# First batch loaded beside the weights, first routed group fetched in the first stage's drain

## What is computed

```python
h = tok_ref(x)                      # x[128, 375, 512]: q, k, v of 125 channels each, softmax over 512
h = h + attn_ref(layernorm(h), Wq, Wk, Wv, Wo)         # 8 heads of 64, 2 of keys and values, rope, tanh cap
h = h + ffn_ref(layernorm(h), gate_w, w1, w2, w3, sw1, sw2, sw3, expert_bias)

def ffn_ref(x, ...):                # 16,000 tokens, 8 experts, top 2, hidden width 448
    scores = softmax(xf @ gate_w); sel = top_k(scores + expert_bias, 2)
    order = argsort(flat_sel, stable=True); token_idx = order // 2
    routed_in = xf[token_idx] * top_scores_sorted[:, None]
    h = silu(ragged_dot(routed_in, w1, counts)) * ragged_dot(routed_in, w3, counts)
    out = silu(xf @ sw1) * (xf @ sw3) @ sw2
    return out.at[token_idx].add(ragged_dot(h, w2, counts))
```

## Time and profile before

| | us |
|---|---|
| median of 3 runs | 5829.84 |
| lowest, highest | 5828.87, 5832.68 |
| the profiled execution | 5829.3 |
| its span | 5827.5 |
| PE busy | 5695.0 (98%) |
| DVE busy | 4158.4 (71%) |
| ACT busy | 3372.5 (58%) |
| POOL busy | 2001.2 (34%) |
| mean granted PE clock | 0.991 of full speed |

### The profile page before, as it was taken

One profiled execution on the slowest core, in us unless ns is written; L12 is line 12 of the kernel. 1 busy time (PEld: TensorE's weight loads), 2 busy tenths in 40 slices (PEclk: granted clock), 3 DMA queues, 4 the chain that ended last, 5 costly groups with the idle time before them and its releaser, 6 DMA issues. The chain is left out here.

```text
span 5827.5 us, 109798 instructions
## 1 busy us (share of the span) xinstructions
PE 5695.0 (98%) x32259; PEld 5030.8 (86%) x32259; DVE 4158.4 (71%) x9591; ACT 3372.5 (58%) x6260; POOL 2001.2 (34%) x1711
## 2 busy tenths in 40 slices
PE   5999999999999999999999997999999999999999
PEld 4888888888888888888888885899999999999998
DVE  3777777777777777777777775676777677667675
ACT  4666666666666666666666663555555555555554
POOL 1333333333333333333333332333333333333333
PEclk8999999999999999999999998999999999999999
DMA  2111111111111111111111111777777777777762
GB/s 74 45 49 48 44 48 49 44 48 49 44 47 50 44 46 50 45 46 50 45 45 50 46 45 45 190 190 188 184 187 189 185 188 188 190 185 186 188 167 80
DMA packets 363663, 565.45 MB, mean 97 GB/s; under 512 B 92898, under 2 KB 187106, under 8 KB 363492
## 3 DMA queue, kind: packets, MB, share of 16 engines
q1 hardware_dynamic: 294276, 433.22, 24.9%
q0 software_dynamic: 69344, 131.70, 11.4%
HBM read 438.14 MB, written 138.42 MB: 99 GB/s over the span
## 5 line engine op out<-in xcount | busy, mean ns | idle before, releaser
L1435 POOL DMA_INDIRECT out_dram<-res,goal x273 | 483.9, 1773 | 1135.8 <-DMA entries<-routed_entries 476.2
L945 POOL TENSOR_TENSOR vT_low<-vT_full,vT_high 128x500 fp32r<-128x500 f32 x128 | 162.6, 1271 | 1576.5 <-ACT vT_high L691 1576.5
L624 ACT ACTIVATE e<-ps,negmax 128x512 f32<-128x512 f32 x512 | 350.6, 687 | 427.4 <-PE ps L437 416.0
L1182 PE MATMUL ps<-rT_hi,up_hi 128*128 128x384 f32 x2548 | 552.2, 338 | 6.5 <-DVE rT_lo L1345 6.5
L1182 PE MATMUL ps<-rT_lo,up_hi 128*128 128x384 f32 x2548 | 551.6, 338 | 0.0
L1182 PE MATMUL ps<-rT_hi,up_lo 128*128 128x384 f32 x2548 | 551.4, 338 | 0.0
L1275 ACT ACTIVATE uT_hi<-egb 128x384 fp32r<-128x384 f32 x364 | 191.4, 526 | 572.0 <-DVE egb L1364 523.6
L966 POOL DMA_INDIRECT routed_entries<-entry,slot x256 | 320.3, 1251 | 468.4 <-DVE slot L906 425.9
L1182 PEld LDWEIGHTS ps<-rT_hi,up_hi 128*128 128x128 f32 x2548 | 457.2, 188 | 14.3 <-issue 6.8
L1182 PEld LDWEIGHTS ps<-rT_lo,up_hi 128*128 128x128 f32 x2548 | 456.1, 188 | 0.0
L1182 PEld LDWEIGHTS ps<-rT_hi,up_lo 128*128 128x128 f32 x2548 | 456.1, 188 | 0.0
(11 more groups left out here) (220 smaller groups left out, 14993.9 us busy)
## 6 DMA issues: line engine op xcount, KB each, us to landing
raw<-in_L_ffn_w SPq DMA_DIRECT2D x182, 768.0 KB, 5.1
X<-in_x SPq DMA_DIRECT2D x128, 750.0 KB
raw<-in_L_ffn_w SPq DMA_DIRECT2D x91, 896.0 KB
raw<-in_L_ffn_w SPq DMA_DIRECT2D x273, 128.0 KB, 5.4
normed_rows<-y SPq DMA_DIRECT2D x128, 250.0 KB
out_dram<-h SPq DMA_DIRECT2D x128, 250.0 KB
rows<-normed_rows,entries POOLq DMA_INDIRECT x273, 4.0
out_dram<-res,goal POOLq DMA_INDIRECT x273
```

Source lines behind the costliest of these rows:

```text
L624: nc.scalar.activation(e[:, i, :], ps[:, (i + 1) % 2, :], ACT.Exp, bias=negmax[:, i:i + 1], accum_out=total[:, i:i + 1]).then_inc(e_sb.sem, 1)
L1182: ins = nc.tensor.matmul(ps[:, bank, 0:GROUP], w[a][:, k, col:col + P], rT[b][:, k, :], start=(k == 0 and i == 0), stop=(k == KC - 1 and i ...
L1435: nc.gpsimd.indirect_dma_start(out, bass.IndirectOffsetOnAxis(ap=goal[group[1] % 2][:, i:i + 1], axis=0), res[i][:], None, bounds_check=la ...
```

## The change

It has two halves, and some buffers move for them.

**Start.** SP's first DMA is now batch 0 of `x`. The loads of the weights follow in the old order, `raw_q` in two DMAs of 512 KB in place of eight of 128 KB, and each weight has a semaphore of its own, so PE and ACT wait for a piece when they need it. The mark for empty entries is stored last, from a smaller tile `blank` that is repeated nine times, on a semaphore `blanked` that POOL waits for ahead of its first scatter in stage one. ACT scales and rounds batch 0 as the first thing in the first block, and POOL cuts it there. Three `memset` of `rows` and the two iotas move to the first block as well.

**Between the stages.** The third block is gone. Its operations on DVE stand at the end of DVE's stage one, in 27 operations in place of 48 (the loop over experts has become four operations on 8 x 91 elements). At step 128 SP waits for the transposes of the last `xn` and loads the weights of expert 0 into `raws`; at the end of stage one it waits for the last writes and scatters and fetches the entries of the first group. POOL gathers the first group's rows there too. In stage two the first group's fetches and gathers are left out, and ACT splits its weights before it scales its rows.

**Buffers.** `raws[0]` and `raws[1]` share a tile `early` with the two X buffers and `xn`; `raws[2]` shares `weights_raw` with `e`. `early<-in_x` below is thus a load of X.

```diff
+        early = sbuf("early", [P, 2 * KC * HID])
+        weights_raw = sbuf("weights_raw", [P, KC, D])
...
+        raws = (early[:, 0:KC * HID].rearrange("p (k h) -> p k h", k=KC),
+                early[:, KC * HID:2 * KC * HID].rearrange("p (k h) -> p k h", k=KC), weights_raw[:, :, :])
...
+        X = [early[:, p * 3 * D:(p + 1) * 3 * D].rearrange("p (a d) -> p a d", a=3) for p in range(2)]
+        xn = early[:, 6 * D:7 * D]
...
+        e = weights_raw
...
-                    for j in range(G):
-                        for g in range(NKV):
-                            load(raw_q[g * HD:(g + 1) * HD, j, :], wq[(g * G + j) * HD:(g * G + j + 1) * HD, :])
+                    sp.dma_start(X[0][0:C, :, :],
+                                 x[0].rearrange("(a c) d -> c a d", a=3)).then_inc(x_in.of((0, 0)), 16)
+                    for g in range(NKV):
+                        sp.dma_start(raw_q[g * HD:(g + 1) * HD, :, :],
+                                     wq[g * G * HD:(g + 1) * G * HD, :].rearrange("(j p) d -> p j d", p=HD)
+                                     ).then_inc(q_in, 16)
...
-                    sp.wait_ge(s_raw, 16 * N_LOADS)
+                    sp.dma_start(routed.rearrange("(p r n) c -> p r n c", p=P, n=BLANK),
+                                 blank[:, None, :, :].to_broadcast([P, REGIONS // P // BLANK, BLANK, ENTRY])
+                                 ).then_inc(blanked, 16)
+                    sp.wait_ge(small_in, 48)
...
+                    pool.wait_ge(qk_hi.sem, qk_hi.at((0, 0)))
+                    nc.gpsimd.tensor_tensor(out=qk_low[0:C, :, :], in0=X[0][0:C, 0:2, :],
+                                            in1=qk_high[0][0:C, :, :].bitcast(F32),
+                                            op=ALU.subtract).then_inc(qk_lo.sem, 1)
...
-                    pe.wait_ge(s_raw, 16 * N_LOADS)
                     pe.wait_ge(s_const2, 2)
-                    for n, (src, _, _) in enumerate(jobs):
+                    for n, (src, _, _, src_in, landed) in enumerate(jobs):
+                        pe.wait_ge(src_in, landed)
...
+                    act.wait_ge(x_in.of((0, 0)), x_in.at((0, 0)))
+                    nc.scalar.activation(X[0][0:C, 0:2, :], X[0][0:C, 0:2, :], ACT.Copy,
+                                         scale=QS).then_inc(x_scaled.sem, 1)
+                    act.wait_ge(x_scaled.sem, x_scaled.at((0, 0)))
+                    nc.scalar.activation(qk_high[0][0:C, :, :], X[0][0:C, 0:2, :], ACT.Copy).then_inc(qk_hi.sem, 1)
...
+                def first_weights():
+
+                    sp.wait_ge(xT_ps.sem, xT_ps.at((0, NB - 1)))
+                    sp.dma_start(raws[0][:], w1[0].rearrange("(k p) h -> p k h", p=P)).then_inc(w_in[0].of((0, 0)), 16)
...
-                    if n == 0:
-                        load(t)
+                    if n == NB:
+                        first_weights()
...
+                    sp.wait_ge(y_out.of(b), y_out.at(b))
+                    sp.wait_ge(scattered.of(b), scattered.at(b))
+                sp.dma_start(entries[0][:], routed[0:GROUP, :].rearrange(
+                    "(p i) c -> p i c", p=P)).then_inc(entries_in.of((0, 0)), 16)
...
+                then(nc.vector.tensor_tensor(by_expert, number[:, None, :].to_broadcast([1, E, NG]),
+                                             upto[:, :, None].to_broadcast([1, E, NG]), ALU.is_ge))
+                then(nc.vector.tensor_reduce(expert_f[:], by_group, AX.X, ALU.add))
...
-                    for i in range(E):
-                        then(nc.vector.tensor_scalar(passed[:], number[:], upto[:, i:i + 1], None, ALU.is_ge))
-                        then(nc.vector.tensor_tensor(expert_f[:], expert_f[:], passed[:], ALU.add))
...
+                        if n == LAG:
+                            pool.wait_ge(blanked, 16)
...
+                pool.wait_ge(entries_in.of((0, 0)), 16)
+                for i in range(T):
+                    nc.gpsimd.indirect_dma_start(
+                        rows[i][:], None, normed, bass.IndirectOffsetOnAxis(
+                            ap=entries[0][:, i, 0:1].bitcast(I32), axis=0),
+                        bounds_check=pool.to_reg(TOKENS - 1), oob_is_err=False).then_inc(rows_in[i], 16)
...
                         if first:
-                            fetch_entries(group)
-                            fetch_weights(group)
                             fetch_entries(back(group, -1))
...
                         if first:
+                            split_up(group, 0)
+                            split_up(group, 1)
                             for i in range(T):
                                 scale_rows(group, i)
-                            split_up(group, 0)
-                            split_up(group, 1)
...
-                    for i in range(T):
-                        nc.vector.memset(rows[i][:], 0.0).then_inc(cleared, 1)
```

More of the change, by code:

```diff
@@ L256, in _ @@
                                              ACT.Copy).then_inc(s_hi, 1)
-                    act.wait_ge(s_raw, 16 * N_LOADS)
-                    for raw, w in direct:
+                    for raw, w, src_in, landed in direct:
+                        act.wait_ge(src_in, landed)
                         nc.scalar.activation(w[0][:], raw[:], ACT.Copy).then_inc(s_hi, 1)
@@ L281, in audio_tower @@
         ve2, rs2 = one("ve2", [P, 1]), one("rs2", [P, 1])
-        xn = one("xn", [P, D])
         xT = parts("xT", [P, KC, P])
@@ L1444, in work @@
                         if first:
-                            for i in range(T):
-                                gather(group, i)
                             for i in range(T):
```

213 lines of the change are left out of this document (104 added, 109 removed).

## The result

The changed kernel takes 5775.99 us (median of 4 runs, 5773.35 to 5779.14), the kernel before, beside it, 5831.26 us (4 runs, 5828.87 to 5835.38). The ratio is 0.9905, with a 95% interval from 0.9888 to 0.9922: 55.3 us less where 47.3 were forecast.

The account below looks back on a forecast made before the run. PE was taken to bound both stages, leaving gaps at the start and between them. Gains of 26.4 (start), 19.1 (between) and 1.8 (clock) sum to 47.3 us: 5829.84 to 5782.5 us, range 5776 to 5790.

Parts of the forecast that it names:

- the price of X for what stands behind it: At the start, raw_q's share on X's DMA engines waits behind X, then needs 2.7 us at 390 GB/s.
- a third of the DMA engines: At the start, X's load uses about a third of the 16 engines: five, by its 125 partitions.
- What bounds the kernel, and the two gaps to work on: PE bounds both stages; the change works only in 59.8 us ahead of stage one and 45.7 us between the stages.
- X landed at 9.7: At the start, batch 0, issued first at 0.79, lands 8.90 us later, at 9.7 us.
- `raw_q` at 12.4: At the start, raw_q is there at 9.7 + 2.7 = 12.4 us; without queueing behind X, by 7.
- Rival 3: At the start, weights arrive late through X's slow engines, raw_2 ending 3 to 6 us later: 5785.5 to 5788.5 us; chance 0.10.
- The block takes 20.65 us from the first transposes: First block, from PE's first transpose to DVE's last operation: 20.65 us as before, so it ends at 33.05.
- Weights and entries fetched in the drain cost nothing: End of stage one: 2.6 MB of first-group weights take 6.7 us and delay nothing anyone waits for.
- 19.1 us between the stages: Between the stages, the shorter chain puts the first product at 3632.7 instead of 3651.76: 19.1 us less.
- The clock stays up, 1.8 us: Start of stage two: PE's clock stays up after the transposes, so products of 3.7 us take 1.9: 1.8 us less.
- Stage two unchanged: Stage two, from first product to end, keeps its 2175.7 us, since no instruction is taken from PE; only the clock's gain.
- rival 5: Slower: moved loops load code each round (5842.5 us at 1 us each), or new buffer addresses cost stage one's batches; chance 0.03.

Follow-up runs that it names:

- e2: The changed kernel with 32 bytes of empty space ahead of stage two's tiles: 5777.57 us, ratio 0.9910 to the kernel before.
- e6: The changed kernel with PE's seven redundant waits of the first block left out: 5778.88 us.
- e14: The changed kernel with 128 bytes of empty space ahead of the tile rT: 5778.33 us.
- e16: The changed kernel with the first load of X split into partitions 0 to 111 and 112 to 124, still ahead of the weights: 5769.45 us.
- e15: The changed kernel with X behind the weights and 128 bytes of empty space ahead of uT alone: 5756.22 us, ratio 0.9873 to the kernel before.

## Why the start gave 16.7 us and not 26.4

The step that failed is the price of X for what stands behind it: `raw_q` was forecast at 12.4 us and came at 21.06. Two theories were set against each other: X ahead of the weights (X), or the shape of `raw_q`'s load, two DMAs in place of eight (Q).

```diff
-                    for g in range(NKV):
-                        sp.dma_start(raw_q[g * HD:(g + 1) * HD, :, :], ...
+                    for j in range(G):
+                        for g in range(NKV):
+                            sp.dma_start(raw_q[g * HD:(g + 1) * HD, j, :], ...
...
```

> The changed kernel with raw_q in eight loads as before, X still first. Theory Q (the new shape of the raw_q loads, four rows 128 KB apart in each partition, is what makes the start's transfers slow): PE's first transposes at about 12.4 us, as I had predicted, first scores at 33.5, time 10 us lower. Theory X (X ahead of the weights slows them): no better, transposes at about 21, scores at 43.

Measured (e3): PE's first transposes at 19.44, first scores at 41.50, 5777.84 us. Q is worth 1.6 us at most, and part of it can be chance: with the start unchanged, PE's first transposes came at 20.13 to 21.06 in five runs (after, e2, e6, e8, e14). Then X was put behind all weights, and ACT's two operations on it behind the splits of the shared expert:

```diff
-                    sp.dma_start(X[0][0:C, :, :], ...)
                     for g in range(NKV):
...
+                    sp.dma_start(X[0][0:C, :, :], ...)
                     sp.dma_start(cos_t[0:C, :], cos).then_inc(small_in, 16)
```

> The changed kernel with the load of X behind the last weight and its rounding on ACT behind the weights' splits; raw_q stays in two loads. Theory X: raw_q is there at about 7, X itself at about 28 (20.5 of weights, 6.3 of its own transfer and 1), and the first scores start at about 33 (X at 28, ACT 2.1, POOL 2.3), 10 us earlier than with X first. Theory Q: raw_q is late here too, transposes at 12 or later, scores at 37 or later.

Measured (e4): 5764.09 us, and in the timeline:

```profile
8.61 1.94 PE L292 MATMUL ps<-ident,raw_q 128*128 128x128 f32 x8 [8.61 <-DMA raw_q<-in_L_attn_Wq]
...
13.39 0.53 SPq L220 DMA_DIRECT2D early<-in_x  x1
...
26.96 1.06 ACT L307 ACTIVATE early<-early 125x1024 f32<-125x1024 f32 x1 [0.42 <-DMA early<-in_x]
...
29.52 2.82 DVE L281 TENSOR_TENSOR w2s_lo<-raw,w2s_hi 64x512 fp32r<-64x512 f32 x1
...
32.81 0.76 PE L503 MATMUL ps<-qk_high 125*128 125x512 f32 x1 [11.90 <-PEq L204]
```

PE starts 12.5 us earlier, the scores 10.3 us. (The 2.1 us between the two are DVE's last operation: it took 2.82 us beside POOL's cut of X, where it takes 0.68 in the change.) X's place is the cause. But what of X? The prediction had given X a third of the DMA engines and let only `raw_q`'s share wait behind it. X itself, issued at 13.39 among other loads, also took 13.6 us here (ACT waited for it at the end), where alone it took 8.90. The last run of this part leaves X first and only spreads it:

```diff
-                    sp.dma_start(X[0][0:C, :, :], ...).then_inc(x_in.of((0, 0)), 16)
+                    sp.dma_start(X[0][0:112, :, :], ...).then_inc(x_in.of((0, 0)), 16)
+                    sp.dma_start(X[0][112:C, :, :], ...).then_inc(x_rest, 16)
...
                     act.wait_ge(x_in.of((0, 0)), x_in.at((0, 0)))
+                    act.wait_ge(x_rest, 16)
```

> The changed kernel with the first load of X split into partitions 0 to 111 and 112 to 124, on two semaphores, still ahead of the weights. Theory S (X of 125 partitions goes over few DMA engines, and 112 goes over all 16): X is in ACT's hands by about 8 us and not at 15.3, PE's first transposes come at 12 us or earlier and not at 21.1, the first scores at 33 to 35 and not at 43.1, time 5767. Theory O (what counts is that 768 KB with rows of 2 KB stand ahead, however they are spread, and that all loads run at half their rate in this stretch): PE's first transposes at 19 us or later, the first scores at 41 or later, 5775.

Measured (e16): 5769.45 us, with this timeline and this rate in slices of 0.65 us, 0 to 26 us:

```profile
6.35 1.28 ACT L302 ACT_TABLE_LOAD   x1 [6.35 <-DMA early<-in_x]
...
6.46 5.05 SPq L220 DMA_DIRECT2D raw<-in_L_ffn_sw  x1
7.65 1.06 ACT L302 ACTIVATE early<-early 125x1024 f32<-125x1024 f32 x1
...
11.20 1.94 PE L294 MATMUL ps<-ident,raw_q 128*128 128x128 f32 x8 [11.20 <-DMA raw_q<-in_L_attn_Wq]
...
33.26 0.77 PE L506 MATMUL ps<-qk_high 125*128 125x512 f32 x1 [9.75 <-PEq L205]
```

```profile
GB/s 0 0 28 101 249 410 315 236 176 271 208 221 236 221 205 208 347 407 410 422 403 396 411 411 344 323 380 386 373 395 388 375 314 229 320 335 293 224 205 146
```

X has landed by 6.35 and not by 15.25, PE has `raw_q` at 11.20 and not at 21.06, the rate is near 400 GB/s from 10 us on, and the scores start at 33.26: theory S, with the same 768 KB still first. The Trainium skill, "DMA: Bandwidth & Descriptors", section "Why a DMA increments its semaphore by 16 and not by 1", says that a transfer goes over the largest number of engines up to 16 that divides the slowest dimension of both its access patterns; 125 gives 5, 112 gives 16. This case agrees: while only loads of X were under way in the kernel before, the 16 engines had a share of 0.32, or 5.1 of them (the first of these rows, with share and GB/s at the end), and the spread load came 8.9 us earlier than the unspread one.

```profile
48.00:54.00 6.00, 0.00 (x0) 0.00 (x0) 0.00 (x0) 0.00 (x0) 0.00 (x0) 0.50 0.32 121
```

What the prediction missed stands in the next three rows: the kernel before, the changed kernel, and the run with X spread.

```profile
12.00:18.00 6.00, 0.00 (x0) 0.00 (x0) 0.00 (x0) 0.00 (x0) 0.00 (x0) 1.00 1.05 382
```

```profile
6.00:18.00 12.00, 0.00 (x0) 0.00 (x0) 0.00 (x0) 2.11 (x2) 0.53 (x1) 1.00 1.07 205
```

```profile
12.00:18.00 6.00, 4.70 (x22) 3.59 (x20) 2.77 (x4) 2.88 (x5) 0.22 (x1) 1.00 1.07 386
```

The other eleven engines were not idle behind X's five. All 16 were as busy in the changed kernel as in the others (1.07 beside 1.05 and 1.07) and moved about half as much, so the same bytes kept them busy twice as long. An estimate from rows: X's own transfer, 768 KB at 124 GB/s or 6.2 us, takes 12.4 us at half the rate, and with the 2.7 us that stood beside it in the 8.90 this makes 15.1; X took 14.5. So the forecast's order, X first and `raw_q`'s share behind it, may well have held, and its rates did not. That X's place and its spread decide is shown by these runs; why the engines slow down while a load on five of them stands ahead of loads on all is not.

## The gap between the stages

Its length was forecast to 0.1 us, out of two errors that cancel. POOL's first gather came 10.5 us after the drain's last product, not 13.5, and the block ended 4.2 us after the third gather, not 0.5. The run below puts the gathers behind the stage's end:

```diff
-                pool.wait_ge(entries_in.of((0, 0)), 16)
-                for i in range(T):
-                    nc.gpsimd.indirect_dma_start(rows[i][:], ...
...
                         if first:
+                            for i in range(T):
+                                gather(group, i)
```

> The changed kernel with the three gathers of the first group moved from POOL's end of stage one to its start of stage two, as they stood before; entries and weights are still fetched ahead. After the last gather at 3601.92 the other engines left stage one only at 3606.12, 4.2 us later. Theory D (POOL's leaving of a stage costs some 4 to 5 us after it has issued indirect DMAs, whichever they are): the last ones are now the scatters at 3592.67 or so, POOL is free by 3598, the stage ends with the tables at 3600.1, ACT starts at about 3600.7 and the gathers are issued from about 3601 on; first rows by 3605, three products' worth of transposes behind ACT's splits: first product at about 3610 to 3611, so 22.5 us between the stages and not 26.7. Theory F (a fixed price of the end of a stage): 4.2 us after the tables' end at 3600.1, ACT starts at 3604.3 and the gathers at 3604.5, first rows at 3608.5, first product at 3613.5: about 25.5 us between the stages. All times are from the span's start, as in the changed kernel. Time 5772 by D, 5775 by F.

Measured (e8): 5773.72 us, 26.94 us between the stages. Its timeline:

```profile
3589.16 1.19 POOL L1069 DMA_INDIRECT routed_entries<-entry,slot  x1 [8.35 <-DVE slot L970]
3590.65 1.19 POOL L1069 DMA_INDIRECT routed_entries<-entry,slot  x1 [0.30 <-issue]
...
3597.80 0.20 DVE L1010 CAST group_row<-row_f 1x91 int32<-1x91 f32 x1
...
3599.43 1.05 POOL L1444 DMA_INDIRECT rows<-normed_rows,entries  x1 [7.58 <-issue]
...
3602.87 0.72 ACT L1281 ACTIVATE rows<-rows,entries 128x512 f32<-128x512 f32 x1 [1.02 <-DMA rows<-normed_rows,entries]
...
3607.89 0.72 ACT L1281 ACTIVATE rows<-rows,entries 128x512 f32<-128x512 f32 x1 [4.30 <-DMA rows<-normed_rows,entries]
```

ACT enters stage two at 3598.57, 0.57 us after the tables' end: the end of a stage has no fixed price of 4 us, by this one comparison it comes from the indirect DMAs that POOL has issued last (theory D for the opening of the stage). In the kernel before, too, the 5.2 us from the last scatter's end (3612.06) to 3617.24 were then probably mostly this and not the scatter's landing: SP saw it landed 2.0 us after its end in the changed kernel. Whether POOL waits for the data or for something of fixed length isn't told apart. The stage opened 5.5 us earlier (12.8 us after the drain's last product, not 18.3), but nothing was won: the second row tile came at 3607.89, 5 us behind the first, with the next group's transfers beside it. Theory D's time for the first product, 4 us earlier, falls with this.

## The two causes used together

X behind the weights, and a gap ahead of `uT` alone, so that the up products keep the distance 64 and the down products get 192:

```diff
+            gap = sbuf("gap", [P, 32], F32, c2)
             uT = [sbuf("uT_hi", ...
```

> The changed kernel with X behind the weights at the start, and 128 bytes of empty space ahead of uT alone, so that the up products keep their distance (64 modulo 256) and the down products get 192. R256: 173.3 ns for an up product, 229.1 for a down product; 4.1 ns for some 36 down products in each of 91 groups are 13 us less than with 233.2, stage two some 2147 us and the time some 5751. R128: 173.3 and 233.2, stage two 2157 to 2159, the time 5764 as with X behind alone.

Measured (e15): 5756.22 us (4 runs, 5754.05 to 5757.59), ratio to the kernel before 0.9873 (0.9857 to 0.9890), so 72 us less than before and some 20 less than the change. Up 173.35, down 229.21 ns, first scores at 32.76:

```profile
3608.20:5755.80 2147.60, 2133.77 (x11727) 2006.11 (x11727) 1506.84 (x2087) 1147.46 (x1630) 805.16 (x541) 1.00 0.70 181
```

Both paces are as the table says, stage two is 2147.6 us long and not 2158.7. The time missed the 5751 expected by 5 us: stage one took 3548.4 us here, 3.4 more than in the run with X behind alone. Over the runs of this case it lies anywhere from 3542.9 to 3549.8 without an edit that would explain it.

## The prediction, step by step

- **What bounds the kernel, and the two gaps to work on:** right. PE had the same work in both stages.
- **X landed at 9.7:** wrong, 15.25. The 8.90 us of the earlier trace rows were those of X alone on its engines; with 5 MB of weights behind it they don't hold.
- **`raw_q` at 12.4:** wrong, 21.06. This is the mis-sized term, 8.7 of the 9.7 us that the start gave less: it was sized at the full rate of 390 GB/s, and the engines moved 205. Rival 3 came nearest (the loads are late because X's engines are the slow ones for each of them), but it sized this at 3 to 6 us, on the last weight, gave it 0.10, and had only X's engines slow where all 16 were.
- **The block takes 20.65 us from the first transposes:** nearly. DVE's last operation ends at 42.66, 21.6 us after them, then 0.46 to the scores. With X spread, the scores come at 33.26, near the forecast's 33.45, but by other terms: `raw_q` at 11.20 and 22.1 us from there.
- **Weights and entries fetched in the drain cost nothing:** right, PE's stage one is no longer than before. The size was taken too low: the six DMAs carry 2.88 MB (the last 64 rows of `w2` go twice), not 2.6, and took 11.7 us from the first issue to the last landing and not 8.9, which still ended 3.9 us ahead of the next write on SP.
- **19.1 us between the stages:** right in the sum (19.0), by errors that cancel: the first gather came 3.0 us sooner, POOL's leaving cost 4.2 us and not 0.4 to 0.6, and from there to the first product it took 8.4 us and not 8.9.
- **The clock stays up, 1.8 us:** wrong. PE idled 1.6 us between transposes and products as forecast, but there was no risen clock to keep: the transposes from 3610.11 on had 0.50 to their end, where those before had brought it up by 3645.5. The products ran at the low clock for some 2.9 us after the first, where it was 3.7; half of the difference, about 0.4 us, is what came of it.
- **Stage two unchanged:** wrong by 17 us, and the largest error. This is the second step that failed, a term put at nothing: the prediction left the stretch at its length because no instruction was taken from PE, and named the new addresses only as a risk for stage one (rival 5), with no row for their price. The change moves `rT` by 1,312 and the weights by 7,520 bytes, which turns a distance of 128 modulo 256 into 64.

In the spans the sum was 7.0 us short: 9.7 too much at the start and 0.1 between the stages, against 15.2 too little in stage two (17.0 beside the clock's 1.8) and 1.5 in stage one. The last microsecond, of 55.3 against 54.3, is how the profiled executions stand to the medians.

## What to carry to other kernels

A change that allocates tiles elsewhere can move the pace of a PE-bound loop by more than one per cent with no instruction changed: compare the start-to-start time of the dominant product in both traces before giving a gain to the edit, and try a few empty gaps of 32 to 192 bytes between the two operands of that product. A load that runs alone on few of the DMA engines, as X did here with its 125 partitions, should not stand ahead of large loads unsplit: split (112 + 13 here) or put last, it gave the start 10 us back. A total that fits can hide terms that cancel: check each link.

## What the runs showed of the hardware

- The pace of stage two's products (float32 parts) depends on the distance between the SBUF addresses of their two operands, modulo 256 bytes or modulo 512: 173.3 to 175.8 ns for 128x384 and 228.2 to 233.5 ns for 128x512. It is the same from run to run to some hundredths of a ns, and moving all tiles of the stage together by 32 bytes changes it little (175.79 to 175.55 for up, 0.4 ns for down) or not at all (the changed kernel).
- In stage one, which holds such products as well, single groups moved by some 4 ns in both directions (the second pass of the shared expert's down product from 233.3 to 230.0, the third pass of its up product from 203.9 to 207.8 ns), with a sum that can't be told from the spread of 7 us of that stage.
- X in one load of 125 partitions, 0.77 MB ahead of 5 MB, cost the first of the loads behind it 9.9 us against the same bytes in the same order, split into 112 and 13 partitions. From 6 to 18 us all 16 engines were busy (share 1.07) and moved 205 GB/s.
- A block that ends behind POOL's indirect DMAs ended 4.2 us after the last issue, and 0.57 us after DVE's last operation where POOL had been done for 6 us.
